# A fused decoder kernel: the first group's Gram products and triangular solve moved into the first phase

## What is computed

```python
q = silu(dwconv(hs @ Wq.T, cq)); k = silu(dwconv(hs @ Wk.T, ck)); v = silu(dwconv(hs @ Wv.T, cv))
beta = sigmoid(hs @ Wb.T)                       # one per head, 4 heads of 64
q, k = l2n(q), l2n(k); v = v * beta; kb = k * beta
# in chunks of tokens (the reference: 32; this kernel: 128, the same recurrence)
A = tril(kb @ k.T, -1)
Tinv = solve_triangular(eye + A, eye, lower=True, unit_diagonal=True)
u = Tinv @ v; w = Tinv @ kb
for chunk in chunks:                            # S: the state, 64 x 64 per head
    attn = tril(q @ k.T); u = u - w @ S; o = q @ S + attn @ u; S = S + k.T @ u
long_ = dwconv31(v); short = dwconv3(v)         # gated mix of short, long_, o and v follows
```

## Time and profile before

| | us |
|---|---|
| median of 3 runs | 1167.36 |
| lowest and highest | 1163.31, 1170.25 |
| span of the profiled execution | 1164.0 |
| its first phase | 0 to about 171 |
| Gram products, solve and long filter of group 0 | about 176 to 217 |
| DVE's first instruction of body 0 | 233.40 |

### The profile page before, as it was taken

The page is one execution under the profiler, slowest core; times in us unless marked ns, Lnnn a source line. Parts: engine busy times, 40 slices in busy tenths (PEclk is TensorE's granted clock), DMA queues, the critical chain, the costliest instruction groups (busy, mean ns, idle before and its releaser), DMA issues.

```text
span 1164.0 us, 25598 instructions
## 1 busy us (share of the span) xinstructions
PE 1010.0 (87%) x9234; PEld 751.0 (65%) x9234; DVE 829.7 (71%) x2173; ACT 528.1 (45%) x992; POOL 603.4 (52%) x1005
## 2 busy tenths in 40 slices
PE   4899979668599899999999989989989979989982
PEld 1565558655476676676676667757767747768871
DVE  2999985853576777787676787687688674557577
ACT  2878763412332542442442443343353336755751
POOL 6977834138115626816816736744762324345542
PEclk9999998769599989999989999989999989999986
DMA  9374451350100150150151152121121353324588
GB/s 201 95 213 151 145 168 62 120 182 19 55 19 29 55 175 25 64 178 34 64 180 37 49 150 77 47 97 56 31 72 38 147 183 102 95 80 146 165 278 307
DMA packets 86795, 127.67 MB, mean 110 GB/s; under 512 B 28304, under 2 KB 62608, under 8 KB 84496
## 3 DMA queue, kind: packets, MB, share of 16 engines
q1 hardware_dynamic: 79472, 106.30, 29.6%
q0 software_dynamic: 7200, 19.74, 4.7%
HBM read 66.47 MB, written 59.55 MB: 108 GB/s over the span
## 4 chain that ended last, share of the span: by engine, by line
PE 46%; POOL 19%; DVE 18%; issue 8%; ACT 4%; DMA 3%; SPq 1%; ACTq 0%; DVEq 0%; POOLq 0%
POOL arena L1522 7%; POOL arena L1524 7%; PE bank L511 3%; PE bank L551 3%; DVE arena L1646 3%; PE bank L952 3%; PE bank L723 3%; PE bank L801 2%; PE bank L791 2%; POOL orn L1540 2%; PE bank L565 2%; PE bank L902 2%; POOL arena L1415 2%; PE bank L430 2%; PE bank L577 2%
## 5 line engine op out<-in xcount | busy, mean ns | idle before, releaser
L1026 ACT ACTIVATE arena<-bank 128x512 f32<-128x512 f32 (+4 forms) x358 | 185.9, 539 | 369.7 <-PE bank L943 69.8
L1584 POOL DMA_INDIRECT results<-arena x78 | 76.5, 980 | 84.8 <-DVE arena L2211 57.9
L1646 DVE SCALAR_TENSOR_TENSOR arena<-arena,param 128x512 f32<-128x512 f32 x144 | 108.1, 767 | 12.5 <-ACT arena L1049 9.0
L1522 POOL TENSOR_TENSOR arena<-arena 128x126 f32<-128x126 f32 (+22 forms) x217 | 91.5, 422 | 39.5 <-DVE arena L1742 24.0
L1524 POOL TENSOR_TENSOR arena<-arena 128x126 f32<-128x126 f32 (+22 forms) x217 | 87.1, 401 | 17.0
L952 PE MATMUL bank<-arena 128*128 128x128 f32 x624 | 85.9, 282 | 0.0
L413 PE MATMUL bank<-const,arena 128*128 128x128 f32 x256 | 38.7, 300 | 54.2 <-DVE arena L2143 28.2
L1486 POOL TENSOR_TENSOR arena<-arena,rb 128x256 f32<-128x256 f32 x32 | 19.9, 623 | 121.0 <-ACT arena L1026 120.7
L1512 POOL COPY arena<-arena 32x128 f32<-32x128 f32 x128 | 50.8, 397 | 58.5 <-DVE arena L1732 52.0
L1462 POOL DMA_INDIRECT slots_x<-arena x64 | 63.3, 989 | 34.3 <-DVE arena L1945 18.5
L952 PEld LDWEIGHTS bank<-arena 128*128 128x128 f32 x624 | 79.2, 199 | 0.3 <-issue 0.3
(11 more groups left out here) (290 smaller groups left out, 2733.7 us busy)
## 6 DMA issues: line engine op xcount, KB each, us to landing
arena<-slots_x SPq DMA_DIRECT2D x78, 129.0 KB, 2.2
slots_x<-rows_of_no_token SPq DMA_DIRECT2D x8, 1161.0 KB, 10.3
xt<-x_in SPq DMA_DIRECT2D x16, 512.0 KB, 6.4
kq_T<-kq SPq DMA_DIRECT2D x8, 1024.0 KB, 4.2
kq<-kq_T SPq DMA_DIRECT2D x8, 1024.0 KB, 7.9
arena<-results SPq DMA_DIRECT2D x32, 256.0 KB, 5.3
arena<-ffn_in SPq DMA_DIRECT2D x7, 768.0 KB, 4.2
vT<-v_T SPq DMA_DIRECT2D x8, 514.0 KB, 4.5
```

Source lines behind the costliest of these rows:

```text
L1026: free(act.activation(out_, in_, func, **kw), name)
L1522: own.link(pool.tensor_tensor(tmp, rows32[:, m0:, k].unsqueeze(2).broadcast_to([P, nm, k]), units[:, 0:k, k].unsqueeze(1).broadcast_to([P, ...
L1584: pool.indirect_dma_start(results[:, :], bass.IndirectOffsetOnAxis(ap=dest[:, n % YS:n % YS + 1], axis=0), ys[:, n % YS, :], None).then_in ...
L1646: ins = V.scalar_tensor_tensor(cv[:, k % 4, :], pre[:, j, d:d + GT], param[:, at + d:at + d + 1], cv[:, k % 4, :], ALU.mult, ALU.add)
```

## The change

Y, the right-hand side of the solve, is not needed before `front_rows(0)`, so its space keeps the keys and queries of group 0 through the first phase (`keys_first`). In groups 3 to 6 of that phase, one tile of group 0's Gram products at a time, PE multiplies after its fourth projection (banks 6 and 7; the projections now turn through banks 2 to 5), DVE scales and masks after `conv(i, 2)`, and POOL copies the diagonal blocks after its `rnorm`. DVE's `front_units(0)` stands at the end of group 6. The substitution is no longer `first_solve` on DVE but `front_steps(0)` on POOL, ahead of `rnorm(NG - 2)` and `rnorm(NG - 1)`. On DVE, `later_scales` moves behind the two turns of the result.

```diff
+        keys_first = Y.rearrange("p a b -> p (a b)").rearrange("p (a b t) -> p a b t", a=2, b=2)
+        def keys_of(i):
+            return kq[i % 2] if i else keys_first
@@ PE
-            proj_bank = cycle((2, 3, 4, 5, 6))
+            proj_bank = cycle((2, 3, 4, 5))
                     project(i, j)
+                    if j == 3 and 3 <= i < 3 + T:
+                        front_gram(0, i - 3, keys_first, (6, 7))
...
-            keys_loaded(0)
-            front_gram(0, 0)
             pe.wait_ge(taps_loaded, 16 * CK * QB)
             pe.wait_ge(sem("v_spread"), 2 * NG)
             for t in range(T):
-                if t:
-                    front_gram(0, t)
                 long_filter(0, t)
@@ POOL
             for i in range(NG):
                 if 0 < i < NG - 1:
                     hidden_rows(i + 1)
-                if i:
+                if 0 < i < NG - 1:
                     rnorm(i - 1)
+                if 3 <= i < 3 + T:
+                    front_diagonals(0, i - 3)
...
             front_solve(0)
-            pool.sem_inc(sem("first_rows_set"), 1)
+            front_steps(0)
+            rnorm(NG - 2)
             rnorm(NG - 1)
             front_rows(0)
@@ DVE
                 for j in range(1, 6):
                     conv(i, j)
+                    if j == 2 and 3 <= i < 3 + T:
+                        front_gram(0, i - 3)
+                if i == 2 + T:
+                    front_units(0)
                 if i + 1 < NG:
                     dve.wait_ge(sem("conv_ready"), 6 * i + 6)
                     halo(i + 1)
...
-            for t in range(T):
-                front_gram(0, t)
-            front_units(0)
-            first_solve()
             front_compact(0)
+            front_natural(0)
+            front_second(0)
             later_scales()
-            front_natural(0)
-            done(V.memset(Tn[0:QB, :, QB:], 0.0), "upper_cleared")
-            front_second(0)
```

More of the change, by code:

```diff
@@ L453, in square_sums, with front_gram @@
                 full(last, n)
+            def front_gram(i, t, src, ks):
+                tt = slice(t * P, (t + 1) * P)
+                o = [open_bank(pe, f"gram{t}{r}.{i}", ks[r]) for r in range(2)]
+                for c in range(CK):
+                    for r in range(2):
+                        rr = slice(DH * r, DH * r + DH)
+                        last = mm(o[r][:, c * 2 * P:(c + 1) * 2 * P], src[rr, c, 0, tt], src[rr, c, :, tt],
+                                  start=True, stop=True)
+                        if c == CK - 1:
+                            full(last, f"gram{t}{r}.{i}")
             hidden_rows(0)
@@ L502, in front_values, with next_gram @@
                 full(last, n)
[L504 to L514, removed]
+            def next_gram(i, t):
+                front_gram(i, t, kq[i % 2], (3, 7))
             def cross(i):
@@ L1065, in square @@
                     filled(act, f"stat.{i - 1}")
-                done(act.activation(sq[:, 2 * (j % 2) + j // 2, :], kq[i % 2][:, j % 2, j // 2, :], ACT.Square),
+                done(act.activation(sq[:, 2 * (j % 2) + j // 2, :], keys_of(i)[:, j % 2, j // 2, :], ACT.Square),
                      "squares_ready")
@@ L1416, in hidden_rows, with front_diagonals @@
                                             ALU.subtract, ALU.mult), "hs_rows_ready")
+            def front_diagonals(i, t):
+                hh = slice(t * H, (t + 1) * H)
+                pool.wait_ge(sem("gram_ready"), HT * i + H * (t + 1))
+                for r in range(NQ):
+                    rr = slice(QB * r, QB * r + QB)
+                    done(pool.tensor_copy(diag[rr, :, hh], A[rr, hh, rr].rearrange("p h j -> p j h")),
+                         "diag_ready")
+                    pool.wait_ge(sem("diag_ready"), HT * i + H * t + r + 1)
             hidden_rows(0)
@@ L1686, in scales, with front_gram, front_units @@
                 dve.sem_inc(sem("scales_ready"), 1)
+            def front_gram(i, t):
+                for r in range(2):
+                    n = f"gram{t}{r}.{i}"
+                    o = filled(dve, n)
+                    ov = o[:, :].rearrange("p (i a c) -> p i a c", i=2, a=2)
+                    for c in range(2):
+                        h = t * H + 2 * c + r
+                        done(V.scalar_tensor_tensor(A[:, h, :], ov[:, c, 0, :],
+                                                    sc[:, i, t, 2 * c + r:2 * c + r + 1],
+                                                    cst("lower"), ALU.mult, ALU.mult), "gram_ready")
+                    free(V.tensor_tensor(attnT[i % 2][:, t * H + r:(t + 1) * H:2, :], ov[:, :, 1, :],
+                                         cst("upper").unsqueeze(1).broadcast_to([P, 2, P]), ALU.mult), n)
+            def front_units(i):
+                dve.wait_ge(sem("diag_ready"), HT * (i + 1))
+                if i:
+                    dve.wait_ge(sem("solved"), i)
+                done(V.transpose(units.rearrange("p (j a) k -> p j (a k)", j=QB),
+                                 diag.unsqueeze(2).broadcast_to([P, QB, 2, HT])), "units_ready")
             for i in range(NG):
@@ L2387, in _ @@
                 sp.wait_ge(sem("act_ready"), 6 * i + 4)
[L2388 removed]
+                done(sp.dma_start(kq_d[i, :, :, :, :], keys_of(i)[:, :, :, :]), f"kq{i % 2}_stored", 16)
                 sp.wait_ge(sem("act_ready"), 6 * i + 6)
```

68 lines of the change are left out of this document (15 added, 53 removed).

## The result

The changed kernel took 1158.4 us (median of 19 runs, lowest 1154.25) beside 1166.18 us for the kernel before (19 runs): ratio 0.9931, 95% interval 0.9915 to 0.9946. That is 8 us faster, where 9.5 was forecast. The time lies in the range; the direction is as forecast. One of the 19 executions of the changed kernel took 1314.44 us at a granted clock of 0.735, where the profiled one had 0.944, and the ratio leaves it out.

What follows compares the result with a forecast made beforehand. DVE was taken to bound the first phase, PE close behind. DVE's first Gram drain in body 0 was to move from 237.20 to 227.7, 9.5 us gained: median 1167.4 - 9.5 = 1157.9 us, range 1150 to 1165.

Steps and rivals of the forecast that it cites:

- Drains, units and the phase: First phase: Gram drains add 7.0 us, POOL's disturbance 0.6, units 1.25, less 0.4; group 7's taps start at 160.9.
- the fourth rival: First phase: bank 7 drained 2 us later in each of four groups, 6 to 8 us lost; 1165, chance 0.09.
- Taps beside POOL: Group 7's 18 taps: one POOL step per tap, each tap waits 0.13 us; DVE loses 2.4 us, POOL 7.9.
- the second rival: Group 7: each tap waits for a whole POOL step, DVE loses 7.2 us instead of 2.4; 1161, chance 0.13.
- PE's wait before the last sums of squares: Before the long filter: sums wait for ACT's square until 176.8, PE idles nearly 8 us, low clock makes sums about 7.
- The sixteen filters: PE's long filter: 16 x 1.78 plus four `front_values` of 0.7 make 31 us, from 183.5 to 214.5.
- The chain to the milestone: From ACT's `front_blocks` at 215.5, 12.2 us to DVE's first drain at 227.7; the bound, later than DVE's 226.3.
- the milestone: DVE empties the first Gram bank of group 1 in body 0: 237.20 before, forecast 227.7, 9.5 us gained.
- Behind the milestone: After DVE's first Gram drain in body 0 everything shifts rigidly, so 9.5 us gained there gives span 1154.5.
- the third rival: Long filter: low clock holds on, each filter 3.63 us instead of 1.78; all sixteen give about 1188; chance 0.05.
- the first rival: Group 7: POOL's steps fit between taps, DVE loses nothing, long filter starts 179 to 181, 13 us gained; 1153, chance 0.17.

Runs made afterwards that it cites:

- the second profile of the changed kernel: Profile of the changed kernel run again with no edit: 1159.66 us beside 1168.46 for the kernel before, ratio 0.9926.
- The kernels with pieces: Changed kernel, group 0's keys reloaded earlier, v and group 1's keys in six 256 KB pieces: 1153.75 us; also with substitution on DVE, units behind phase: 1154.60.
- the kernel with POOL's half alone: Kernel before with only the substitution moved to POOL; Gram products, diagonals and units stay behind the phase: 1175.49 us beside 1168.46, ratio 1.0073.

## Why the prediction was right, and where it was not

I hold it against the second profile of the changed kernel, where group 3 starts as in the kernel before.

- **Drains, units and the phase.** Right. The taps of group 7 start at 160.63; the sum said 160.9. PE waited for bank 7 in one of the four groups, for 0.34 us before beta in group 3, and never for a projection's bank; so four banks and bank 7 cost nothing to be seen in the taps' start, and the fourth rival is out.
- **Taps beside POOL.** Right in mechanism, too dear: 0.07 us a tap instead of 0.13, 1.0 us for fifteen instead of 2.0. The last spread ended at 180.04, not 181.6. POOL lost 6.3 us, not 7.9, and took one step a tap, as forecast. By the second rival each tap would have been 0.4 us longer; the traces show 0.07, and it is out. The Trainium skill, SBUF — State Buffer, section Who interferes with whom, has the rule behind that rival, that whoever comes first keeps the shared ports for its whole instruction. The traces agree with it on POOL's side, not on DVE's.
- **PE's wait before the last sums of squares.** Mis-sized. I had 176.8, 8 us idle; it was 173.51 after 4.68. The square that it waits for came 7.1 us later than before, and I had moved it by 8.5 + 1.9. The low clock was there as forecast, and the sums took 6.4 us instead of 3.84. The filters began at 180.3, 3.2 us before my 183.5, and it was the spread that released them (after 0.38 us of idle), not the sums.
- **The sixteen filters.** This is the term that failed. I had 31 us from durations of before and said nothing of the reload, which I knew to be on SP's queue; I had asked what hides the filters' own cost but not what the 2.5 MB would now lie on. They took 35.5: 2.4 of stop, and the rest mostly the low clock behind it. The kernels with pieces took 31.2 and 32.0, so the 31 was right for filters alone.
- **The chain to the milestone.** From `front_blocks` to DVE's first drain 13.2 us instead of 12.2; 0.70 of the difference is one more short stop of PE, before 224.43, and a 16 KB transfer had left 2.3 us earlier, at 222.15. The bound is the one I named: DVE was ready at 226.8 and waited 3.10 us for PE. Milestone 229.9 against 227.7: late by 4.5 for the filters, early by 3.2 for their start, late by 1.0 here. Two errors of opposite sign covered each other by luck, which is why 8 us came of 9.5. It is luck too that the forecast of 1157.9 us lies so near 1158.4: it stood on a kernel before of 1167.4, which the 19 runs put at 1166.18.
- **Behind the milestone** I had taken everything to shift rigidly. The first profile bears it out: 3.3 us gained at the milestone, 3.6 at POOL's first step, 3.0 at the end. The second doesn't: 7.3, 7.0 and 10.1. In it PE came back from the low clock sooner in body 0 (granted clock 0.90 in the window of 70 to 80 us behind the milestone, against 0.63 in the first profile and 0.59 in the kernel before), and PE's first Gram product of body 1 followed the milestone by 88.5 us, against 90.7 and 91.2. Two executions of one kernel differ by that much, so one profile can't tell what is gained behind the milestone. In the kernel with POOL's half alone 9.9 us lost at the milestone were 6.1 at the end. The long filter at the low clock throughout (the third rival) did not occur.

Of the first rival, the small contention was true and the early clock was not.

## What to carry to other kernels

When a change lets an engine run where it used to wait for a transfer, ask what else that transfer is in the way of: it is still there, and its new neighbour may be the engine's own program. What helped here was to send the bulk loads beside PE's thousands of short instructions in pieces of 256 KB, paced by PE's progress, and not in one of 1 MB. And try the halves of a two-part change apart: here one carried all of it, and the other, alone, was 7 us slower than nothing.

## What the runs showed of the hardware that I had not expected

- The 16 KB transfers that I take for PE's instructions wait behind bulk loads: with the DMA engines full or nearly so (share 0.84 to 1.02) they left 3.7 to 4.0 us late, and PE stopped for 2.4 to 3.1 us. A fetch 1.5 us late in one kernel stopped it as long (1.31) as one 2.6 us late in another (1.30), so how much delay PE can bear differs from place to place; what it depends on was not tried.
- In these runs a stop of 2.4 us or more was followed by the 1.2 GHz level, and both stops of 1.3 us were not.
- DVE's taps, with two inputs from SBUF each, and small steps of POOL share the time unevenly: DVE gave 0.07 us an instruction, POOL up to 0.5 a step.
- Between executions of one kernel, group 3 started at 82.50 once and at 78.66 once: DVE had the rows of x at 63.17 and at 60.27, and in the first a stretch at the low clock followed. A single profile can be 4 us off for that alone.
